# Mean squares of a layer norm: four turned blocks and ScalarE sums against four products with a column of 1/512

## The reference, cut to what matters

```
def hypergraph_conv(x, adj, W, b):
    H = (adj != 0).astype(x.dtype)
    w = adj.reshape(N, -1)[:, :C]
    xw = jnp.einsum('ncd,hd->nch', x, W)
    ...
    m = Be[:, :, None] * jnp.einsum('nce,nch->neh', H, xw)
    out = Dn[:, :, None] * jnp.einsum('nce,neh->nch', H, m)
    return out + b
h = jax.nn.relu(hypergraph_conv(x, adj, W1, b1))
h = layer_norm(h, gamma, beta)
y = hypergraph_conv(h, adj, W2, b2)
x = _layernorm(x + (y + x))
```

## Time and profile before

| | us |
|---|---|
| median of 3 runs | 283.41 (283.38 to 283.72) |
| the profiled execution | 283.37 |
| its span in the trace | 281.6 |
| PE busy | 273.6 (97%) |
| PEld busy | 249.5 (89%) |
| DVE busy | 229.5 (82%) |
| ACT busy | 197.3 (70%) |
| POOL busy | 136.0 (48%) |

### The profile page before, as it was taken

How to read it: one execution, slowest core, us unless ns; L and a number is a source line. 1 busy time by engine, 2 the same in 40 slices (tenths; PEclk the granted TensorE clock), 3 DMA queues, 4 the chain that set the end, 5 groups by cost and what they waited for, 6 DMA issues and landing times.

```text
span 281.6 us, 5797 instructions
## 1 busy us (share of the span) xinstructions
PE 273.6 (97%) x1820; PEld 249.5 (89%) x1820; DVE 229.5 (82%) x648; ACT 197.3 (70%) x561; POOL 136.0 (48%) x199
## 2 busy tenths in 40 slices
PE   7999999999999999999999999999999999999991
PEld 6889889898999989898998989899898989989891
DVE  3795689797878979797897979798897969798884
ACT  3588967776777787777768877676787765574723
POOL 2242546436363644536274553627355353637643
PEclk9999999999999999999999999999999999999998
DMA  6913041335324434432433533443333232110033
GB/s 213 328 55 84 3 130 40 93 113 132 115 57 133 92 93 117 130 114 64 147 72 94 137 109 112 63 147 52 100 91 95 77 113 74 40 57 21 1 112 112
DMA packets 37302, 27.70 MB, mean 98 GB/s; under 512 B 10060, under 2 KB 35352, under 8 KB 37272
## 3 DMA queue, kind: packets, MB, share of 16 engines
q1 hardware_dynamic: 37024, 27.17, 34.0%
q10 hardware_dynamic: 248, 0.17, 0.2%
HBM read 17.21 MB, written 8.42 MB: 91 GB/s over the span
## 4 chain that ended last, share of the span: by engine, by line
PE 90%; ACT 4%; DVE 3%; issue 1%; POOL 1%; POOLq 0%; DVEq 0%; ACTq 0%
PE bank_v L318 31%; PE bank_g L335 10%; PE bank_g L328 10%; PE bank_g L330 10%; PE bank_v L296 9%; PE bank_v L359 8%; PE bank_s L276 4%; PE bank_g L347 3%; PE bank_s L359 1%; PE bank_s L434 1%; ACT ht_sb L533 1%; ACT sq_sb L591 1%; PE bank_g L415 1%; DVE bn_sb L1000 1%; DVE w_lo L844 0%
## 5 line engine op out<-in xcount | busy, mean ns | idle before, releaser
L1049 POOL TENSOR_TENSOR xb_sb<-x_sb,b_half 128x512 f32<-128x512 f32 x32 | 41.2, 1291 | 69.6 <-DVE r_lo L774 50.1
L584 ACT ACTIVATE r_sb<-bank_v,vec 128x512 f32<-128x512 f32 x64 | 44.1, 689 | 39.5 <-PE bank_v L318 38.8
L328 PE MATMUL bank_g<-w_hi,r_hi 128*128 128x258 f32 x256 | 67.0, 294 | 0.0
L330 PE MATMUL bank_g<-w_lo,r_hi 128*128 128x256 f32 x256 | 63.7, 281 | 0.0
L1057 POOL TENSOR_SCALAR r_hi<-r_sb 128x512 fp32r<-128x512 f32 x64 | 44.0, 688 | 39.2 <-ACT r_sb L584 38.7
L318 PE MATMUL bank_v<-u_lo,w_hi 128*128 128x512 f32 x128 | 50.8, 397 | 0.0
L318 PE MATMUL bank_v<-u_hi,w_lo 128*128 128x512 f32 x128 | 50.8, 397 | 0.0
L318 PE MATMUL bank_v<-u_hi,w_hi 128*128 128x512 f32 x128 | 50.7, 396 | 0.0
L328 PEld LDWEIGHTS bank_g<-w_hi,r_hi 128*128 128x128 f32 x256 | 48.3, 189 | 1.7 <-DVE w_lo L844 0.3
L774 DVE TENSOR_TENSOR r_lo<-r_sb,r_hi 128x512 fp32r<-128x512 f32 x64 | 48.7, 782 | 0.9 <-POOL r_hi L1057 0.9
L330 PEld LDWEIGHTS bank_g<-w_lo,r_hi 128*128 128x128 f32 x256 | 48.2, 188 | 1.2
(11 more groups left out here) (127 smaller groups left out, 460.0 us busy)
## 6 DMA issues: line engine op xcount, KB each, us to landing
x_sb<-in_x_dram SPq DMA_DIRECT2D x16, 512.0 KB, 3.9
out_dram<-z_sb SPq DMA_DIRECT2D x14, 512.0 KB, 3.3
adj_sb<-in_adj_dram SPq DMA_DIRECT2D x15, 256.0 KB, 4.1
d_row<-d_rows SPq DMA_DIRECT2D x13, 256.0 KB, 3.5
w_raw<-in_L_gnn_W_dram SPq DMA_DIRECT2D x2, 512.0 KB, 4.8
out_dram<-z_sb SPq DMA_DIRECT2D x3, 256.0 KB, 2.1
adj_sb<-in_adj_dram SPq DMA_DIRECT2D x2, 128.0 KB, 2.3
turned_h<-h_sb SPq DMA_TRANSPOSE x13, 2.4
```

Source lines behind the costliest of these rows:

```text
L328: pe.matmul(bank_g[:, n, 0:W2COLS], r_hi[:, i % 2, k, graph(n)], w2_hi[:, k], start=(k == 0), stop=False)
L330: pe.matmul(bank_g[:, n, 0:DOUT], r_hi[:, i % 2, k, graph(n)], w2_lo[:, k], start=False, stop=False, skip_group_check=True)
L584: nc.scalar.activation(r_sb[:, k], bank_v[:, k % 2], ACT.Relu, bias=vec[:, k:k + 1]).then_inc(relu_ready, 1)
L1049: nc.gpsimd.tensor_tensor(xb_sb[:, i % 2, part], x_sb[:, i % 3, part], b2_half[:, :].unsqueeze(1).to_broadcast([P, n, DOUT]), ALU.add).the ...
```

## The change

The turned blocks, ACT's four sums, and the arrays `scratch` and `sum_sq` go. In their place PE multiplies each graph's block of `q_sb` (stationary, 128x128, fp32) with a column of 1/512 (`hid_share`, streamed, one column). The result, one column of mean squares on the nodes' partitions, goes to column 258 (`MEAN_SQ`) of the same graph's bank. `make_var1` reads all three columns from that bank. The products stand after graph 1 (graphs 0 and 1), after graph 2 and after graph 3; in round 0 the first three stand together after graph 2.

```diff
+        MEAN_SQ = DOUT + 2
...
-        turned_q = bank_g[:, PER - 1]
...
             def make_g(i, n):
-                if n == PER - 1:
-                    pe.wait_ge(q_summed, 2 * i + 2)
...
-            def turn_q(i):
+            def sum_squares(i, graphs_here):
+
                 pe.wait_ge(q_ready, i + 1)
-                pe.wait_ge(q_summed, i * 2)
-                pe.wait_ge(g_ready, i * 2)
-                for n in range(PER):
-                    mm = pe.transpose(turned_q[:, graph(n)], q_sb[:, graph(n)], ident[:, :])
-                mm.then_inc(q_turned, 1)
+                for n in graphs_here:
+                    pe.matmul(bank_g[:, n, MEAN_SQ:MEAN_SQ + 1], q_sb[:, graph(n)],
+                              hid_share[:, :], start=True, stop=True).then_inc(q_summed, 1)
...
                 make_g(i, 0)
-                if 0 < i < LAST:
-                    turn_q(i)
...
-                if i == LAST:
-                    turn_q(i)
-                elif i:
+                if i:
+                    sum_squares(i, each(0))
+                if 0 < i < LAST:
                     make_v(i + 1, 0)
                 make_g(i, 2)
+                sum_squares(i, [2] if i else range(3))
                 if i == 0:
-                    turn_q(0)
...
                 make_g(i, 3)
+                sum_squares(i, [3])
...
-            def sum_q(i):
-                act.wait_ge(q_turned, i + 1)
-                if i:
-                    act.wait_ge(var1_ready, i * 2)
-                for n in range(PER):
-                    ins = nc.scalar.activation(scratch[:, n], turned_q[:, graph(n)], ACT.Copy, scale=1.0 / HID,
-                                               accum_out=sum_sq[:, n:n + 1])
-                    if n % 2:
-                        ins.then_inc(q_summed, 1)
...
             def make_var1(i, half):
                 part, done = graphs(half), i * 2 + half
                 dve.wait_ge(g_made, done + 1)
-                dve.wait_ge(q_summed, done + 1)
-                for n in each(half):
-                    ins = nc.vector.scalar_tensor_tensor(out=stat1[:, 0, n:n + 1], in0=bank_g[:, n, MEAN:MEAN + 1],
-                                                         scalar=bank_g[:, n, MEAN + 1:MEAN + 2],
-                                                         in1=sum_sq[:, n:n + 1], op0=ALU.mult, op1=ALU.add)
+                dve.wait_ge(q_summed, (done + 1) * 2)
+                for n in each(half):
+                    ins = nc.vector.tensor_scalar(stat1[:, 0, n:n + 1], bank_g[:, n, MEAN:MEAN + 1],
+                                                  bank_g[:, n, MEAN + 1:MEAN + 2],
+                                                  bank_g[:, n, MEAN_SQ:MEAN_SQ + 1], ALU.mult, ALU.add)
...
             def add_pairs(i):
                 dve.wait_ge(pairs_ready, i * 2 + 2)
                 if i:
-                    dve.wait_ge(q_turned, i)
+                    dve.wait_ge(q_summed, i * PER)
...
+            nc.gpsimd.memset(hid_share[:, :], 1.0 / HID)
```

More of the change, by code:

```diff
@@ L46, in hypergraph_block @@
         ident_2 = sb("ident_2", [P, P])
+        hid_share = sb("hid_share", [P, 1])
         half_power = sb("half_power", [P, PER])
@@ L89, in hypergraph_block @@
         q_sb = sb("q_sb", [P, PER * P])
-        scratch = sb("scratch", [P, PER, P])
-        sum_sq = sb("sum_sq", [P, PER])
         stat1 = sb("stat1", [P, 2, PER])
@@ L143, in hypergraph_block @@
         r_hi_ready, r_lo_ready, pairs_ready = sem("r_hi_ready"), sem("r_lo_ready"), sem("pairs_ready")
-        q_ready, q_turned, q_summed = sem("q_ready"), sem("q_turned"), sem("q_summed")
+        q_ready, q_summed = sem("q_ready"), sem("q_summed")
         g_made, stat1_step, var1_ready, rstd1_ready = sem("g_made"), sem("stat1_step"), sem("var1_ready"), sem("rstd1_ready")
@@ L676, in _ @@
                     normalise(i - 1, 0)
-                sum_q(i)
                 if i == LAST:
@@ L979, in make_last_var1 @@
                 dve.wait_ge(last_g_made if n == 2 else g_made, 1 if n == 2 else G * 2)
[L980 to L983, removed]
+                dve.wait_ge(q_summed, LAST * PER + n + 1)
+                nc.vector.tensor_scalar(stat1[:, 0, n:n + 1], bank_g[:, n, MEAN:MEAN + 1],
+                                        bank_g[:, n, MEAN + 1:MEAN + 2], bank_g[:, n, MEAN_SQ:MEAN_SQ + 1], ALU.mult,
+                                        ALU.add).then_inc(last_step, 1)
                 dve.wait_ge(last_step, n - 1)
```

## The result

The changed kernel takes 290.61 us (290.54 to 290.81, 6 runs) against 283.40 for the kernel before: a ratio of 1.025, with a 95% interval of 1.024 to 1.027. It is slower by 7.2 us. The forecast was 289.5 with a range of 287.2 to 291.9.

The account below looks back on a forecast made before the run. The prediction took PE's stream to bound rounds 1 to 14. Net +0.40 us a round gave +5.6, round 0 +0.28 and round 15 +0.25: +6.1 on 283.37, so 289.5 us, range 287.2 to 291.9.

Parts of the forecast that it names:

- What bounds the kernel: Rounds 1 to 14: PE's stream sets the time, 16.20 us busy in a 16.20 us round; relieving ACT gives nothing.
- The record at 0.11 us: PE, middle rounds: each load-and-product pair costs 0.11 us, so four one-column fp32 products, eight records, add 0.88 us a round.
- The turned blocks at 0.48: PE, middle rounds: removing the turned blocks saves 0.48 us a round, their switch in and out included.
- Round 0: First round: three products replace the turned blocks, v starts 0.06 us later, graph 3's product adds 0.22; together +0.28 us.
- Round 15: Last round: ACT drops out of the chain, but DVE's graph 3 step waits for PE's products; +0.25 us.
- By columns (a): PE's products: priced by streamed columns, the loads vanish; -6.3 us, ends near 277, or 279 with the issue floor; chance 0.07.
- the short load (b): PE's products: the load is as short as the turned blocks', 0.06 us a record; net 0, about 283.4 us; chance 0.06.
- No overlap at all (c): PE's products: each record costs its load's whole 0.19 us; 1.04 us a round, 299 us; chance 0.05.
- The new wait (d): make_var1 on DVE: its new form or wait uses up the 1.5 us of cover; 296 us or more; chance 0.03.
- The price for small products: PE's products by the skill's issue floor of about 25 ns: eight records 0.20 us, some 3.9 us faster over 14 rounds.

Follow-up runs that it names:

- the kernel without products: The changed kernel with the four mean-square products left out, the variance taking the constant 1/512 instead: 277.79 us.
- cols128: The changed kernel, but each mean-square product streams 128 columns of 1/512 instead of one: 291.37 us.
- bf16one: The changed kernel with q_sb and the column in bf16 and all four products of a round in one block: 280.42 us.
- bf16: The changed kernel with q_sb and the column in bf16, the products still in three blocks: 283.36 us.

## Why the prediction was right, and where it was short

**What bounds the kernel** held: PE had no gap in a middle round of any of the kernels run, and the time followed PE's stream in each.

**The record at 0.11 us** held: eight records cost 0.91 us a round by the kernel without products, against 0.88 forecast. The 0.03 left is a matter of size, 0.91 / 8 = 0.114 where 0.11 stood; the block edges make 0.01 of it. The reason, the load, is borne out in three places. 127 columns more cost 0.01 (cols128). The loads follow one another at (0.53 - 0.19) / 3 = 0.11 in the row at 128.91 (last section). And records with a short load take 0.03 (bf16one). The first load of a block starts with the last product ahead of it (128.91), and v's load is exposed in its place: that is the shift of one record that the prediction counted among the eight. What isn't shown is an fp32 product whose block stays loaded, so a price that fp32 and fp32r share for another reason than their load isn't ruled out.

**The turned blocks at 0.48** were mis-sized: the kernel without products gives 0.44. The row that misled is in the timeline above: graph 0's four L332 take 0.51 us to the next product (127.08 to 127.59) where graph 1's take 0.48, and no turned block follows them any more; the kernel without products has the 0.51 as well. That 0.03 was in the 1.91 us of the earlier trace rows and I had booked it on the turned blocks. It stays with the change. What graph 0's last products wait for wasn't tried.

These two make 0.47 a round where 0.40 stood. Over rounds 1 to 14 that came to 6.49 us (230.67 from the start of round 1 to that of round 15, against 224.18 before) where 5.6 stood: 0.9 of the 1.1 us between forecast and result.

**Round 0** came out at +0.24 against +0.28, the start of round 1 moving from 42.26 to 42.50, and v's load starting at 29.47, as forecast. But the agreement doesn't confirm the price: the kernel without products starts round 1 at 42.49 too, with its wait of 1.0 us for `u_lo` where the first three products would stand. What else holds it back in round 0 wasn't followed.

**Round 15** came out dearer: its start moved by 6.73 us (266.44 to 273.17 in the two traces) and the span by 7.2, so about 0.5 instead of 0.25. The chain of the changed kernel there:

```profile
280.11 0.13 PE bank_g L343 x2
280.24 0.03 issue
280.29 0.05 issue
280.34 0.30 DVE stat L965
```

ACT is gone from this chain and graph 3's product stands at its head, as forecast. DVE's step for graph 3 (L965) follows L981 of the earlier trace rows 280.34 - 273.31 = 7.03 us later, 0.30 beyond the start of the round. The rest comes behind it: the new DVE form takes 0.30 in the chain where L981 took 0.14. Over the whole trace it has a mean of 280 ns, where the old one took 0.34 for two. The third PSUM column isn't the reason: the same form with `hid_share` from SBUF in its place has 275 ns in the kernel without products. The forecast covered that form in the middle rounds, where it costs nothing, and left it out at the end.

**The rivals.** By columns (a) and the short load (b) fell with cols128 and with the loads' 191 ns. No overlap at all (c) would have needed 0.19 between loads. The new wait (d) shows up, `make_var1` waits for PE's products 17.5 us in all where it waited 11.9 for `make_g` before, but no `g_sb` is among PE's waits.

**The price for small products.** The Trainium skill ("TensorE: Matmul & The Clock Gate", section "Back-to-back issue gap") names an issue floor of about 25 ns for small products. By the prediction's estimate from it the change would have been 3.9 us faster. The traces show where it can be met: in bf16one v's first product starts 0.11 us after the first of the four bf16 products, 0.03 for each (the rows at 141.83 and 141.94). For fp32 they show 0.11 for each load instead.

## What to carry to other kernels

A product with a single streamed column isn't small. In fp32 a block of one, two or four of them cost 0.23, 0.44 and 0.89 us here, two loads of 0.11 for each product: the first load ran beneath the product ahead, and the load of what stood behind the block was exposed instead, since nothing streamed under which it could run. In bf16 the products' own loads all but vanished, and the 0.11 of the load behind was left, once for each block. So count loads, by type, before trading other work for such products; let the stationary block be bf16 where the accuracy allows; and put bf16 products side by side, so that a neighbour's load is exposed once. And where one engine's stream sets the time, as PE's does here, work taken from an engine that it doesn't wait for was worth nothing.

## What the runs showed of the hardware

A bf16 load didn't run beneath the fp32r product ahead of it. In bf16 the last of the four L332 starts near 159.02 + 3 x 0.12 = 159.38 and the bf16 load at 159.50, 0.12 later; in the changed kernel the fp32 load starts at 128.91, together with the last L332 (128.55 + 3 x 0.12):

```profile
128.91 0.53 PEld L343 LDWEIGHTS bank_g<-hid_share,q_sb 128*128 128x128 f32 x4
129.36 0.19 PEld L317 LDWEIGHTS bank_v<-u_hi,w_hi 128*128 128x128 f32 x1
```

Both hold for every block of the two traces but that of round 0, where PE waits for `q_sb`. What it costs isn't shown: the bf16 product itself starts at 159.50, 0.12 behind the last L332, and that is the distance of the L332 from each other. Whether another order of the kinds would let the load start earlier wasn't tried.
